# GNN stack on one core: where the attention stage reads a tile's destination values, and how far ahead its one-hots run

## The reference

```python
h = (x @ W).reshape(n, H, C)
a_src = (h * att_src).sum(-1)
a_dst = (h * att_dst).sum(-1)
alpha = a_src[src] + a_dst[dst]
alpha = jnp.where(alpha >= 0, alpha, NEG_SLOPE * alpha)
m = jax.ops.segment_max(alpha, dst, num_segments=n)
ex = jnp.exp(alpha - m[dst])
denom = jax.ops.segment_sum(ex, dst, num_segments=n)
alpha = ex / denom[dst]
msg = h[src] * alpha[..., None]
out = jax.ops.segment_sum(msg, dst, num_segments=n).reshape(n, HC) + bias
```

## Time and profile before

| | us |
|---|---|
| median of three runs | 5707.21 |
| lowest and highest | 5705.53, 5707.76 |
| profiled execution | 5708.69 |
| span of its records | 5706.8 |
| PE busy | 4036.3 (71%) |
| POOL busy | 3982.9 (70%) |
| DVE busy | 3649.0 (64%) |
| ACT busy | 1865.0 (33%) |

### The profile page before, as it was taken

One profiled execution on the slowest core, in us unless ns is written; L12 is line 12 of the kernel. 1 busy time (PEld: TensorE's weight loads), 2 busy tenths in 40 slices (PEclk: granted clock), 3 DMA queues, 4 the chain that ended last, 5 costly groups with the idle time before them and its releaser, 6 DMA issues.

```text
span 5706.8 us, 119109 instructions
## 1 busy us (share of the span) xinstructions
PE 4036.3 (71%) x24045; PEld 3010.9 (53%) x24046; DVE 3649.0 (64%) x10855; ACT 1865.0 (33%) x5770; POOL 3982.9 (70%) x3352
## 2 busy tenths in 40 slices
PE   3666539999267777777577777777773788888884
PEld 3555528888245555555355555555552455555553
DVE  5676786667844444444655555555554688888886
ACT  0000011212011111111365666665562344444442
POOL 4767787772067777777288888888884477777771
PEclk6555555555555555555788888888886899999997
DMA  5666526654042322222144444444444444544441
GB/s 118 190 187 191 162 81 177 177 174 124 3 131 72 73 73 73 73 74 72 12 35 35 35 35 36 36 36 36 35 36 76 118 134 133 135 135 134 134 133 39
DMA packets 396078, 536.69 MB, mean 94 GB/s; under 512 B 86434, under 2 KB 273900, under 8 KB 396001
## 3 DMA queue, kind: packets, MB, share of 16 engines
q0 software_dynamic: 213152, 301.19, 27.7%
q1 hardware_dynamic: 134897, 125.62, 7.3%
q10 hardware_dynamic: 47952, 109.14, 6.7%
HBM read 408.63 MB, written 127.00 MB: 94 GB/s over the span
## 4 chain that ended last, share of the span: by engine, by line
POOL 22%; PE 20%; issue 18%; DMA 18%; DVE 17%; ACT 3%; SPq 1%; DVEq 1%; ACTq 1%; POOLq 0%
POOL ACCB L468 15%; DMA acc_dram<-GR,ARENA 12%; PE WIDE L621 9%; POOL acc_dram L477 5%; DMA ARENA<-p_dram,SRCI 4%; POOL ARENA L494 3%; DVE ACCB L1021 3%; DVE ARENA L1203 2%; DVE ARENA L1021 2%; PE WIDE L730 2%; PE WIDE L557 2%; DVE T L1021 2%; PE WIDE L712 1%; DVE ARENA L1554 1%; ACT GR L818 1%
## 5 line engine op out<-in xcount | busy, mean ns | idle before, releaser
L477 POOL DMA_INDIRECT acc_dram<-GR,ARENA x830 | 1283.3, 1546 | 351.2 <-ACT GR L818 220.8
L460 POOL DMA_INDIRECT GR<-h_dram,SRCI x830 | 942.3, 1135 | 342.3 <-issue 244.0
L494 POOL DMA_INDIRECT ARENA<-p_dram,SRCI x830 | 866.6, 1044 | 302.8 <-issue 154.4
L468 POOL DMA_INDIRECT ACCB<-h_dram,SRCI x830 | 864.5, 1042 | 274.3 <-issue 252.1
L659 PE MATMUL WIDE<-ACCB 128*128 128x128 f32 x1660 | 634.1, 492 | 333.2 <-DMA ACCB<-h_dram,SRCI 278.8
L818 ACT ACTIVATE ACCB<-WIDE (+2 forms) x1667 | 641.5, 385 | 390.2 <-PE WIDE L789 327.4
L730 PE MATMUL WIDE<-ACCB 128*128 128x128 f32 x3320 | 596.1, 309 | 234.4 <-issue 234.4
L730 PEld LDWEIGHTS WIDE<-ACCB 128*128 128x128 f32 x3320 | 543.9, 220 | 391.1 <-issue 283.5
L776 PE MATMUL WIDE<-W1es,GR 128*128 128x320 f32 x1660 | 633.0, 464 | 148.3 <-DVE ARENA L1021 119.7
L818 ACT ACTIVATE ARENA<-WIDE 128x40 f32 (+3 forms) x525 | 197.2, 376 | 1580.4 <-PE WIDE L677 571.2
L1463 DVE SCALAR_TENSOR_TENSOR ACCB<-WIDE,ARENA,ACCB 128x128 f32<-128x128 f32 x1660 | 568.1, 351 | 185.4 <-ACT ACCB L929 170.0
(11 more groups left out here) (316 smaller groups left out, 6605.1 us busy)
## 6 DMA issues: line engine op xcount, KB each, us to landing
T<-pairs_dram ACTq DMA_DIRECT2D x167, 320.0 KB, 4.0
g_dram<-GR SPq DMA_DIRECT2D x166, 320.0 KB
ACCB<-g_dram ACTq DMA_DIRECT2D x166, 320.0 KB
ARENA<-src_rows_dram SPq DMA_DIRECT2D x166, 160.0 KB, 3.1
GR<-h_dram,SRCI POOLq DMA_INDIRECT x830
ACCB<-h_dram,SRCI POOLq DMA_INDIRECT x830, 2.9
acc_dram<-GR,ARENA POOLq DMA_INDIRECT x830
GR<-in_attr SPq DMA_DIRECT2D x830, 16.0 KB
```

The lines of the kernel that those rows point to most:

```text
L460: pool.indirect_dma_start(GR[:, q, :], None, h_dram[:, :], row_of(j)).then_inc(landed[q], 16)
L468: pool.indirect_dma_start(GX[:, q, :], None, h_dram[:, :], row_of(j)).then_inc(l1_landed[q], 16)
L477: pool.indirect_dma_start(acc_dram[q % NACC][:, :], bass.IndirectOffsetOnAxis(ap=SCI[:, j:j + 1], axis=0), GR[:, q, :], None, compute_op=A ...
L494: pool.indirect_dma_start(HC3[:, j % RING3, :], None, p_dram[:, :], bass.IndirectOffsetOnAxis(ap=SRCI[:, j:j + 1], axis=0)).then_inc(lande ...
```

## The change

ACT takes over the reading of the destination tiles. A new function a_stage loads the five tile numbers of a half-step into ACT's registers and copies, slot by slot, the three parts of that tile's eight columns (24 bf16 numbers a partition) into a ring ADNS of four half-steps. It runs two half-steps ahead. PE reads ADNS at fixed addresses: it has no registers to load, its small matmuls need no address arithmetic, and its loop is now made by by_groups with four half-steps an iteration. PE waits for one more event, a_staged. The one-hots OTB and HIA have four buffers in place of two, and DVE makes them two half-steps ahead: one-hot of m+2, then pick of m. The one-hot of half-step m now waits for pick m-4, whose buffer it takes, and the pick of m waits for pick m-1.

```diff
-        OTB = carve(spread, 4 * HALF * P, 2, HALF * 2 * P)
-        OTP = carve(spread, 4 * HALF * P, 2, HALF, 2, P)
-        HIA = carve(spread, 8 * HALF * P, 2, HALF, NT)
+        OTB = carve(spread, 0, ABUFS, HALF * 2 * P)
+        OTP = carve(spread, 0, ABUFS, HALF, 2, P)
+        HIA = carve(spread, 8 * HALF * P, ABUFS, HALF, NT)
+        ADNS = carve(spread, 9 * HALF * P, ABUFS, HALF, 3, 8)
...
-            with pe.Fori(0, ITER) as i:
-                ts = tile_registers(ENG.PE, i)
-                for h in range(2):
-                    n = i * 2 + h + 1
-                    pe.wait_ge(ev("a_onehot"), n + ABUFS)
-                    pe.wait_ge(ev("a_picked"), n)
-                    pe.wait_ge(ev("a_adas_copied"), n)
-                    for k in range(HALF):
-                        for part in range(3):
-                            pe.matmul(bank(h)[:, k * NT * HEADS:(k + 1) * NT * HEADS], OTP[:, h, k, 1, :],
-                                      ADNB[:, part, :, HEADS:2 * HEADS], start=(part == 0), stop=(part == 2))
-                        for part in range(3):
-                            last = pe.matmul(bank(2 + h)[:, k * 8:(k + 1) * 8], OTP[:, h, k, 0, :],
-                                             ADNB[:, part, bass.ds(ts[h * HALF + k], 1), :].rearrange("p a b -> p (a b)"),
-                                             start=(part == 0), stop=(part == 2))
-                    last.then_inc(ev("a_values"), 1)
+            def a_values(i, g):
+
+                h, n = g % 2, i * LONG + g + 1
+                pe.wait_ge(ev("a_onehot"), n + ABUFS)
+                pe.wait_ge(ev("a_staged"), n)
+                pe.wait_ge(ev("a_picked"), n)
+                pe.wait_ge(ev("a_adas_copied"), n)
+                for k in range(HALF):
+                    for part in range(3):
+                        pe.matmul(bank(h)[:, k * NT * HEADS:(k + 1) * NT * HEADS], OTP[:, g, k, 1, :],
+                                  ADNB[:, part, :, HEADS:2 * HEADS], start=(part == 0), stop=(part == 2))
+                    for part in range(3):
+                        last = pe.matmul(bank(2 + h)[:, k * 8:(k + 1) * 8], OTP[:, g, k, 0, :],
+                                         ADNS[:, g, k, part, :],
+                                         start=(part == 0), stop=(part == 2))
+                last.then_inc(ev("a_values"), 1)
+
+            by_groups(pe, a_values)
...
+            def a_stage(i, b):
+
+                ts = tile_registers(ENG.Activation, i, b * HALF, ABUFS * HALF, HALF)
+                for k in range(HALF):
+                    last = copy(ADNS[:, b, k, :, :], ADNB[:, :, bass.ds(ts[k], 1), :].rearrange("p c a b -> p c (a b)"))
+                last.then_inc(ev("a_staged"), 1)
...
             for b in range(ABUFS - 1):
                 a_rows(0, b)
+            act.wait_ge(ev("slots_loaded"), 32)
+            for b in range(2):
+                a_stage(0, b)
             with act.Fori(0, GROUPS // ABUFS) as i:
                 for b in range(ABUFS):
                     ahead = b + ABUFS - 1
                     a_rows(i + ahead // ABUFS, ahead % ABUFS)
+                    a_stage(i + (b + 2) // ABUFS, (b + 2) % ABUFS)
                     a_adas(i, b)
...
             def a_onehot(i, b):
 
-                h = b % 2
+                m = i * ABUFS + b
                 v.wait_ge(ev(f"a_rows_landed{b}"), i * 16 + 16)
-                v.wait_ge(ev("a_picked"), i * ABUFS + b + 1)
+                if not isinstance(i, int) or m >= 2:
+                    v.wait_ge(ev("a_picked"), m - 1)
...
                 v.wait_ge(ev("a_values"), n + 1)
+                v.wait_ge(ev("a_picked"), n + 2)
...
-            a_onehot(0, 0)
+            for b in range(2):
+                a_onehot(0, b)
             with v.Fori(0, GROUPS // ABUFS) as i:
                 for b in range(ABUFS):
-                    a_onehot(i + (b + 1) // ABUFS, (b + 1) % ABUFS)
+                    a_onehot(i + (b + 2) // ABUFS, (b + 2) % ABUFS)
                     a_pick(i, b)
-            a_onehot(GROUPS // ABUFS, 1)
-            a_pick(GROUPS // ABUFS, 0)
-            v.wait_ge(ev("a_picked"), 2 * ITER + 1)
-            a_pick(GROUPS // ABUFS, 1)
+            for b in range(2):
+                a_pick(GROUPS // ABUFS, b)
```

More of the change, by code:

```diff
@@ L1186, in a_onehot @@
             def a_onehot(i, b):
-                h = b % 2
+                m = i * ABUFS + b
                 v.wait_ge(ev(f"a_rows_landed{b}"), i * 16 + 16)
-                v.wait_ge(ev("a_picked"), i * ABUFS + b + 1)
-                ts1(OTB[:, h, :], BCAST[:, b, :], pcol[:, 0:1], ALU.is_equal)
-                tt(HIA[:, h, :, :], iotab[:, 0:NT].unsqueeze(1).broadcast_to([P, HALF, NT]),
-                   HIC[:, bass.ds((i * ABUFS + b) * HALF, HALF)].unsqueeze(2).broadcast_to([P, HALF, NT]),
+                if not isinstance(i, int) or m >= 2:
+                    v.wait_ge(ev("a_picked"), m - 1)
+                ts1(OTB[:, b, :], BCAST[:, b, :], pcol[:, 0:1], ALU.is_equal)
+                tt(HIA[:, b, :, :], iotab[:, 0:NT].unsqueeze(1).broadcast_to([P, HALF, NT]),
+                   HIC[:, bass.ds(m * HALF, HALF)].unsqueeze(2).broadcast_to([P, HALF, NT]),
                    ALU.is_equal).then_inc(ev("a_onehot"), 1)
@@ L1199, in a_pick @@
                 v.wait_ge(ev("a_values"), n + 1)
+                v.wait_ge(ev("a_picked"), n + 2)
                 tt(PICK, bank(h)[:, 0:HALF * NT * HEADS].rearrange("p (k t c) -> p k t c", k=HALF, c=HEADS),
-                   HIA[:, h, :, :].unsqueeze(3).broadcast_to([P, HALF, NT, HEADS]), ALU.mult).then_inc(ev("a_masked"), 1)
+                   HIA[:, b, :, :].unsqueeze(3).broadcast_to([P, HALF, NT, HEADS]), ALU.mult).then_inc(ev("a_masked"), 1)
                 v.wait_ge(ev("a_masked"), n + 1)
```

## The result

The changed kernel took 5611.42 us, the median of four runs (5602.21 to 5620.6); the kernel before took 5706.37 in the same comparison. The ratio is 0.9835 with an interval of 0.9823 to 0.9847: 95 us faster, where 70 were forecast. The profiled execution took 5608.26 us with a span of 5606.4.

What follows compares the result with a forecast made beforehand. PE's sequencer, by its register load, was taken to bound the attention stage; 2.9 us half-steps save 103 us there, but gathers end the sum stage at 1371 against 1440.72, 70 us earlier: 5707.2 - 70 = 5637 us, range 5615 to 5672.

Steps and rivals of the forecast that it cites:

- PE's load bounds the attention stage, not the DVE: Attention stage: PE's TENSOR_LOAD of ten tile numbers, median 1982 ns, fills the gap between iterations that the label gives DVE.
- so their 2.2 us stay: PE, attention stage: matmuls unchanged in number and size, so they keep 2.2 us of a half-step of about 2.5 us.
- A half-step of 2.9 us: Attention stage: the largest of PE 2.5, DVE 2.63 and ACT 2.75 us, plus 0.17; saves 103 us over 166 half-steps.
- whose cover was to cost nothing: ACT's row broadcast, issued three half-steps ahead, has over 4.5 us to land: covers the 4.0 us median, not 5.9.
- the copies: ACT, attention stage: copies of 128x24 put at 0.17 us each, four of them added to ACT's half-step of 2.77 us.
- The 0.17 us for hiccups: Attention stage: added to the half-step because the same reckoning of the kernel before gave 3.35 us where 3.52 was measured.
- The gathers take over the end: First sum stage: POOL's gathers end it, capping the gain at 70 us of the attention stage's 103; chance 0.62.
- That leaves 420 gathers and the last at 1349: First sum stage: at 1.40 us a gather in the attention stage, 420 remain at 1.50 us each, the last at 1349.
- From the last gather to the end, 22.2 us: First sum stage: store issue 3.5 us later, about 4 us to land, 14.7 us from load to end: 1371.
- The gathers speed up: Rival: DVE idling for rows or fewer store waits bring attention-stage gathers to 1.30 us; gain 103 us, 5604; chance 0.05.
- ACT as the bound at 3.1 to 3.4 us: Rival, attention stage: ACT's load plus five copies set the half-step; at 3.28 us gain 40 us, 5667; chance 0.16.
- Slower gathers in the attention stage: Rival: gathers there take 1.50 us, 443 are left at 718, the last at 1383; gain 36 us, 5671; chance 0.09.

Runs made afterwards that it cites:

- the aligned loads: Changed kernel with every ACT register load begun at a multiple of four, taking five to eight numbers: 5612.03 us, ratio 0.9846.
- The larger ring: Changed kernel with 15 places in place of 10 for POOL's gathered rows, so a gather waits for an older store: 5578.45 us, ratio 0.9796.
- the compares with one operand: Changed kernel with the first sum stage's source-lane one-hot made by five one-operand compares in place of one TENSOR_TENSOR: 5615.76 us, ratio 0.9843.

## Why the prediction was right or wrong

**PE's load bounds the attention stage, not the DVE.** Right, and shown by undoing each half of the change and by the 0.36 us from the load's end to PE's start. One term of PE's sum was wrong: "so their 2.2 us stay" does not hold, since the thirty matmuls of a half-step last 1.80 us without the register operations between them (2.20 before, and 2.20 again where the load is back on PE). PE was not the limit any more, so the forecast did not feel it.

**A half-step of 2.9 us.** Too long; it is 2.69. That ACT sets the pace was right: it hardly waits, and DVE, put at 2.63 us a round, takes 2.45 in the median when it does not wait. In the attention stage (150 to 500 us, 131 half-steps) DVE waits for neither PE nor ACT, but for ACT's broadcasts, whose cover was to cost nothing:

```profile
DVE ACCB L1040 <- DMA T<-pairs_dram: 20.7, 40, 1.3
```

The mis-sized term is the copies: 0.12 us each in place of 0.17, 0.2 us for four. The 0.17 us for hiccups measured 0.10: 30 of 153 loads took more than 1.25 us. Together these are 0.27 us, where 0.23 was missed; the other terms came out 0.04 us higher. The load's 1137 ns had been read rightly from the earlier trace rows. The Trainium skill, page "DMA: Bandwidth & Descriptors", section "Latency and other measured facts", gives about 600 ns as the floor of tensor_load: the shortest load here (542 ns) is a little below it, the median nearly double. Over 166 half-steps the miss was 35 us for the stage and cost the forecast nothing, because of the next point.

**The gathers take over the end.** Right, and the rows foretold for it came: the last gather (1328.0), store and load are within 5.2 us, ACT waits for stores, 17 times and 100.5 us in all, and DVE for the loaded rows (waits of the sum stage: us in total, times, longest):

```profile
ACT T L822 <- DMA g_dram<-GR: 100.5, 17, 6.3
...
DVE ACCB L1036 <- DMA ACCB<-g_dram: 80.2, 38, 4.5
```

Before, DVE hardly waited for rows (821 to 1426 us):

```profile
DVE ACCB L1021 <- DMA ACCB<-g_dram: 4.5, 14, 0.5
```

That a still shorter stage would gain no more is confirmed by the aligned loads, from 2.69 to 2.54 us a half-step. In the attention stage a gather came every 1.43 us where 1.40 was taken. Of the signs, two were just missed: the half-step is a little under the 2.7 to 3.0 us foretold, and gaps of PE reach 1.3 us where under 1 was foretold.

**The step that failed: "That leaves 420 gathers and the last at 1349", at 1.50 us each.** With the 452 gathers that were in fact left at 673 us, 1.50 us each would have ended at 1351, two microseconds from the forecast: the length of the attention stage and the count had no part in the miss, the price alone had. Measured, they took 655 us, 1.45 each, and the last began at 1328. That is 21 of the 25 us between the forecast end of 1371 and the measured 1346.3. The price was taken from a stage in which DVE hardly waited for rows. Once the gathers set the end, DVE does wait: 80 us, of which 72 come after 1220 us, and then a gather is cheaper. POOL's timeline there in the changed kernel, and DVE's beside it:

```profile
1302.31 0.94 POOL L461 DMA_INDIRECT GR<-h_dram,SRCI  x1 [0.30 <-issue]
1303.56 1.39 POOL L461 DMA_INDIRECT GR<-h_dram,SRCI  x1 [0.31 <-issue]
1305.25 0.94 POOL L461 DMA_INDIRECT GR<-h_dram,SRCI  x1 [0.30 <-issue]
1306.50 0.94 POOL L461 DMA_INDIRECT GR<-h_dram,SRCI  x1 [0.30 <-issue]
1307.75 0.94 POOL L461 DMA_INDIRECT GR<-h_dram,SRCI  x1 [0.30 <-issue]
1308.99 0.94 POOL L461 DMA_INDIRECT GR<-h_dram,SRCI  x1 [0.30 <-issue]
1310.24 1.52 POOL L461 DMA_INDIRECT GR<-h_dram,SRCI  x1 [0.30 <-issue]
```

```profile
1302.57 0.82 DVE L1036 TENSOR_TENSOR ACCB<-ACCB,ARENA 128x640 f32<-128x640 f32 x1 [4.19 <-DMA ACCB<-g_dram]
1303.32 0.82 DVE L1036 TENSOR_TENSOR ACCB<-iota,DLC 128x640 f32<-128x640 f32 x1
1304.05 0.82 DVE L1036 TENSOR_TENSOR T<-iotab,LOC 128x640 bf16<-128x640 bf16 x1
1304.79 0.28 DVE L1036 TENSOR_TENSOR T<-iotab,HIC 128x125 bf16<-128x125 bf16 x1
1309.38 0.83 DVE L1036 TENSOR_TENSOR ACCB<-ACCB,ARENA 128x640 f32<-128x640 f32 x1 [4.32 <-DMA ACCB<-g_dram]
1310.13 0.82 DVE L1036 TENSOR_TENSOR ACCB<-iota,DLC 128x640 f32<-128x640 f32 x1
```

The gathers at 1303.56 and 1310.24 start during a DVE operation and take 1.39 and 1.52 us; the five others start while DVE idles and take 0.94. The length goes by what is left of that operation: the one that runs at 1303.56 ends at 1304.14, and the gather ends 0.81 us later. In the sum stage of the changed kernel 263 gathers started with more than 0.14 us of a DVE operation left, and 258 of them ended 0.80 to 0.84 us after its end; in the kernel before it was 235 of 240. So a gather waits out the operation in which it starts, and not the ones behind it.

All gathers sorted by what DVE was doing at their start: in the kernel before 98 of 340 started in its idle time, after the change 182 of 452, and every one of these 280 took under 0.96 us. The mean of the others is (411.0 - 98 x 0.943) / 242 = 1.317 us before (the earlier trace rows has the 411.0) and (520.5 - 182 x 0.943) / 270 = 1.292 us after. So the price of a hindered gather hardly changed; the share of unhindered ones rose from 29% to 40%: it was 33% of the 370 gathers up to 1221 us and 73% of the 81 behind them, while loads waited for stores. The groups of POOL, first in the kernel before (860 to 1330 us), then after the change (700 to 1180, then 1200 to 1328):

```profile
L460 POOL DMA_INDIRECT GR<-h_dram,SRCI x314 | 375.3, 1195 | 95.7 <-issue 95.7
```

```profile
L461 POOL DMA_INDIRECT GR<-h_dram,SRCI x329 | 381.8, 1161 | 100.3 <-issue 100.3
```

```profile
L461 POOL DMA_INDIRECT GR<-h_dram,SRCI x95 | 100.2, 1055 | 28.9 <-issue 28.9
```

With the issue these are 1.50, 1.47 and 1.36 us. While loads waited for stores the 81 gathers came 1.33 us apart, which is some 13 us of the 23 saved against 1.50 each. This part comes back in every kernel in which loads waited like this (1.30 to 1.34 us from start to start). The early part, some 9 us, varies: 1.47 to 1.52 over the five of them that keep the one-hots' work, and what sets it from run to run stays open. The larger ring is the counter-test: there rows are in time, a gather costs 1231 ns, and DVE hardly waits for them:

```profile
DVE ACCB L1058 <- DMA ACCB<-g_dram: 3.4, 10, 1.0
```

The Trainium skill, page "SBUF — State Buffer", section "SBUF: two separate sides", says that a POOL operation that reads SBUF and a DVE operation with two SBUF inputs lock each other out of a shared port pair, and that whichever starts first holds it for its whole length. The traces agree with one side of that, since a gather waits until the operation in which it starts is over. The other side they do not show: 160 DVE operations of 128x640 that started during a gather begun in DVE's idle time took 0.83 us at most, as elsewhere (one is the row at 1309.38).

**From the last gather to the end, 22.2 us.** Measured 18.3: the store was issued 2.9 us after it, its landing took 2.2 us and not the 4 us taken from the broadcast, and from the load to the end it was 13.1 us, not 14.7. This is the other 4 us.

**The rivals.** "The gathers speed up" named the cause, a DVE that idles for rows, but put its effect into the attention stage and gave it 0.05; it belonged into the forecast itself, since the forecast was that DVE would wait. ACT as the bound at 3.1 to 3.4 us: ACT is the bound, but at 2.69, where the gathers cap the gain, since its copies pipeline. Slower gathers in the attention stage: they came to 1.43 us, by the waits for stores (56 of 436 us, has 36 of 400), while their duration went only from 964 to 978 ns. Gathers that start there during the reduce or the masking, which reads PSUM, took 0.94 to 0.95 us on average; only those in the two one-hot operations, of about 0.28 and 0.58 us, took 1.02 to 1.04.

## What to carry to other kernels

An idle time that carries another engine's name can be the engine's own sequencer's, above all when the engine named was itself waiting: look for register loads in the gap, see whether the work always resumes at the same distance from the load's end, then undo one half of the change. An engine with the smallest busy share (here ACT) can be the one that sets the pace. Where removing a bound hands the end to a second one, reckon the second one's price in the state it will then be in: here DVE, waiting for the gathers, no longer hindered them. And once the gathers set the end, more buffers ahead of them (fifteen rows for ten, 33 us) were worth more than a further shortening of the stage beside them (nothing).

## What the runs showed of the hardware

**A register load's length went by its start and its count.** ACT's loads of five numbers took about 0.55 us in the median where the first number's place in the table was a multiple of four, and 1.14 elsewhere; some took up to 2.4. When all started at such places, the medians were 0.55 us for five numbers, 0.77 for six, 0.98 for seven and 0.56 for eight. The earlier trace rows has both lengths, as least and median; the prediction counted with both and had no rule for them.

**A register operation ahead of each small matmul cost PE 0.4 us a half-step.** Thirty matmuls with fifteen such operations took 2.20 us, without them 1.80, at the same granted clock (0.50, the 1.2 GHz level).

**Small copies pipeline on ACT.** A copy of 128x24 lasts 0.21 us and the next starts 0.12 us later, with a register operation between them.

**A row gather costs 0.94 us on POOL, and waits out the DVE operation in which it starts.** It ended 0.82 us after that operation in 258 of 263 cases of the sum stage, where most of DVE's operations last 0.82 us. The one-hots of the attention stage and the compares with one operand held gathers in the same way; the reduce and the masking that reads PSUM did not.
